# Q and K of a gated cross-attention layer kept in DRAM by units of a batch, and the bulk loads of its attention phase issued by ScalarE

## The chip, the cores and the metric

The kernel runs on one core of a Trainium2 chip. The metric is the time of one execution on the device, in microseconds. The kernel before takes 879.33 us, the median of 3 runs (877.48 to 880.64).

## The reference

A gated cross-attention layer and a feed-forward layer with LoRA experts, in float32: 8 batches of 128 tokens, width 512, 32 heads of 128.

```python
h = rmsnorm(layernorm(x)) * ln_weight                      # x: 8 x 128 x 512
q, k, v = h @ w_q.T, ctx @ w_k.T, ctx @ w_v.T              # each 8 x 128 x (32 heads x 128)
score = softmax(where(mask, q k^T + position_bias, -inf))  # per batch and head, 128 x 128
attn = (score v) @ w_out.T                                 # 4096 -> 512
x = x + tanh(g_xattn) * (layernorm(x) + attn)
n = layernorm(x)
x = x + tanh(g_ffn) * (n @ base_W.T + base_b + 2 * top-8 routed LoRA experts(n))
```

## The kernel before

Each float32 operand is split into a high and a low part, and a product is three matmuls (low x high, high x low, high x high). The work has three phases.

*Projections (0 to about 330 us).* 32 jobs (`JOBS`), 16 for K and 16 for Q, each for two heads. The first two are plain; in the others seven block products (`m1` to `m7`, 42 matmuls) make four quarters of a result, R11, R21, R12, R22, each for one head and one half of the batches. ScalarE makes the high part of a quarter in `unit_out`, VectorE the low part, and SyncE's `store(i, n)` (L320) writes it to `qk_units` in DRAM; `st[i]` counts these stores. There are 128 stores of 512 KB. One quarter holds, for each of the 128 partitions, 4 batches x 256 floats (high and low of 128 tokens).

*Attention (about 318 to 830 us).* 64 units: a unit is one batch with a group of 4 heads; unit t = 8g + b is batch b of group g. `load_unit(g, b)` (L353) fetches Q and K of a unit, 1 MB, into one of two buffers `qk`. TensorE's step for unit t makes the scores of t (8 matmuls into Sb), V of t+1 (12 matmuls), the output of t-4 (12), and applies the probabilities of t-2 to V (8 matmuls into Ab, which read `P_hl`). The probabilities are transposed by way of DRAM: VectorE normalises (`p_norm`) and transposes 32 x 32 blocks (`p_blocks`); `store_blocks` (L337) writes them to `p_rows`, `load_blocks` (L343) reads them back in four DMAs into `pT`; ScalarE and POOL split `pT` into `P_hl`. ScalarE's step for unit t (L795) is A_hi and small_a of t-3, V_hi of t, P_hl of t-2 (which waits for `pT`), one split of a weight chunk for the next group, and the four exponentials of t. `load_wv` and `load_wo` fetch W_v and W_o of the next group, one of eight chunks in each unit.

*Feed-forward (about 790 to 882 us).* It begins within the last group: VectorE and POOL make the second layer norm, and the weights (`loraR`, `loraB`, `base`) are split in `late_high` and `late_low`.

All engines are programmed in order, each by its own list, and wait on semaphores. All DMAs are issued by SyncE, in program order: for each unit it waits for p_blocks of t-1 and stores them, waits for the scores of t and loads unit t+2, waits for the stored rows and issues the four reads of `pT`, then one chunk of W_v or W_o. The first units have their own order (`first_units`, L406).

Of the kernel before, what the change touches and what calls it, by code (L numbers as in the profile page):

```python
# [13 lines left out]
P = 128  # L14
# [37 lines left out]
def build(nc, x, ctxT, mask, g_xattn, g_ffn, bias, lnw, wqk, wv, wo, baseT, base_b, loraR, router_b,  # L52
          lora_B, expert_map, qk_units, p_rows, out):
    with ExitStack() as ctx:
# [254 lines left out]

        @block.sync  # L310
        def _(sp):
# [8 lines left out]
            def store(i, n):  # L320
# [6 lines left out]
            def load_wv(g, q, k):  # L327
                if k == 0:
                    reached(sp, v_done, B * (g - 1))
                sp.dma_start(v_raw[q][:, k, :], wv[g, :, k, :]).then_inc(ld_wv[k], 16)  # L330

            def load_wo(g, q, k):
                if k == 0:
                    reached(sp, o_done, B * (g - 1))
                sp.dma_start(o_raw[q][:, k, :], wo[g, :, k, :]).then_inc(ld_o[k], 16)
# [13 lines left out]
            def load_bias(g, q):  # L349
                reached(sp, bm_done, B * (g - 1))  # L350
                sp.dma_start(bias4[:, q, :, :], bias[g, :, :, :]).then_inc(ld_bias, 16)
# [17 lines left out]
            load_bias(0, 0)  # L369
# [5 lines left out]
            for n in range(JOBS + 1):  # L375
# [5 lines left out]
                if n == 19:  # L381
                    for k in range(4):
                        sp.wait_ge(t_lo_done[k], 2)
                    for k in range(DC):
                        load_wv(0, 0, k)
                    for k in range(HU):
                        load_wo(0, 0, k)
                if n >= JOBS - 2 and n < JOBS:
# [3 lines left out]
                    load_unit(0, n % 2)  # L392
# [13 lines left out]
            def first_units():  # L406
                for i in range(4):
                    sp.wait_ge(st[i], 16 * (G + 2))
                sp.wait_ge(scores_done, 1)
                load_unit(0, 2)  # L410
                store_blocks(0, 0)
                load_blocks(0, 0)
                sp.wait_ge(scores_done, 2)
                load_unit(0, 3)
                store_blocks(0, 1)
                load_blocks(0, 1)
                sp.wait_ge(scores_done, 3)
                load_unit(0, 4)
                store_blocks(0, 2)
                load_blocks(0, 2)  # L420
                sp.wait_ge(m_done[4], J(JOBS - 1))
                load_wv(1, 1, 0)
                sp.wait_ge(scores_done, 4)
                load_unit(0, 5)
                load_wv(1, 1, 1)

            def group(g, q):
                first, last = (isinstance(g, int) and g == n for n in (0, GROUPS - 1))
                for b in range(4 if first else 0, B):
                    if first and b == 7:  # L430
                        for i in range(4):
                            sp.wait_ge(st[i], 16 * JOBS)
                    before = (g, b - 1) if b > 0 else (g - 1, B - 1)
                    store_blocks(*before)
                    if not (last and b >= B - 2):
                        sp.wait_ge(scores_done, B * g + b + 1)
                        load_unit(g + (b + 2) // B, (b + 2) % B)
                    load_blocks(*before)
                    if 2 <= b <= 5 and not last:
                        load_wv(g + 1, 1 - q, b - 2)  # L440
                    if b >= 6 and not last:
                        load_wo(g + 1, 1 - q, b - 6)
                    if b < 2 and not first:
                        load_wo(g, q, b + 2)
                    if b == (4 if first else 1) and not last:
                        load_bias(g + 1, 1 - q)
# [190 lines left out]
        def _(act):  # L637
# [205 lines left out]
            for n in range(PLAIN, JOBS + 1):  # L843
# [41 lines left out]
                if n == JOBS - 1:  # L885
                    exponentials(0)
# [916 lines left out]
```

## Time and profile before

| | |
|---|---|
| profiled execution | 884.5 us |
| its span, granted clock | 882.3 us, 0.984 |
| TensorE (PE) busy | 847.7 us (96%) |
| VectorE (DVE) busy | 699.9 us (79%) |
| ScalarE (ACT) busy | 494.7 us (56%) |
| GpSimd (POOL) busy | 496.1 us (56%) |
| DMA | 155392 packets, 214.72 MB, mean 243 GB/s |

PE counts as busy from the start of a matmul to its modelled end, and matmuls overlap; whether a stretch is tight is seen from the distance of their starts. The longest wait of any engine is ScalarE's before P_hl, for `pT`: 124.7 us in 60 times.

### The profile page before, as it was taken

What the parts mean: (1) busy time and instruction counts of PE and PEld (TensorE: products, weight loads), DVE (VectorE), ACT (ScalarE), POOL (GpSimd) and SP (SyncE); (2) the same over time, 40 slices, a digit from 0 to 9 for tenths busy, and PEclk for the clock granted to TensorE, in tenths of its full rate; (3) what the DMA queues carried; (4) which work ended last, traced back from release to release, by engine and by line L of the source; (5) the groups of instructions that cost most, each with busy time, mean ns of one, the idle gap of its engine ahead of it and who ended that gap; (6) DMA issues with size and microseconds to landing.
All of it is one profiled execution on the core that took longest, in us unless ns stands there. A gap on an engine that the chain in (4) does not pass through costs nothing.

```text
span 882.3 us, 13927 instructions
## 1 busy us (share of the span) xinstructions
PE 847.7 (96%) x4212; PEld 712.1 (81%) x4212; DVE 699.9 (79%) x1172; ACT 494.7 (56%) x1185; POOL 496.1 (56%) x352
## 2 busy tenths in 40 slices
PE   7999999999999998889999999999999999987898
PEld 5887888778888887778888888888888888876786
DVE  6888777877766666568888889889988989899664
ACT  6566776666676753456555555555555555546210
POOL 0353534653465532557576776777667666757422
PEclk9999999999999999899999999999999999999799
DMA  8876677579777785987988888898898898884001
GB/s 291 309 280 246 249 276 274 215 294 360 275 299 274 274 309 156 284 270 227 259 230 264 241 249 255 249 259 252 250 257 246 251 260 253 273 262 140 25 25 72
DMA packets 155392, 214.72 MB, mean 243 GB/s; under 512 B 10960, under 2 KB 109392, under 8 KB 154960
## 3 DMA queue, kind: packets, MB, share of 16 engines
q1 hardware_dynamic: 155344, 214.13, 75.6%
q8 instruction: 24, 0.39, 0.2%
q14 instruction: 24, 0.20, 0.1%
HBM read 128.11 MB, written 85.98 MB: 243 GB/s over the span
## 4 chain that ended last, share of the span: by engine, by line
PE 32%; DMA 24%; DVE 24%; ACT 7%; issue 5%; SPq 4%; POOL 1%; DVEq 0%; ACTq 0%; POOLq 0%
DMA pT<-p_rows 11%; DMA p_rows<-p_blocks 10%; DVE p_norm L1128 6%; PE Sb L1417 4%; PE Sb L1418 4%; PE Sb L1419 4%; ACT p_exp L773 4%; SPq L346 4%; DVE unit_out L950 2%; PE Ab L1417 2%; PE Ab L1418 2%; PE Ab L1419 2%; DVE p_blocks L1134 2%; DVE rscale L1123 2%; DMA v_raw<-wv 2%
## 5 line engine op out<-in xcount | busy, mean ns | idle before, releaser
L495 POOL TENSOR_TENSOR w_lo<-w_raw,w_hi 128x1280 fp32r<-128x1280 f32 (+1 forms) x29 | 84.8, 2924 | 122.7 <-ACT w_hi L639 122.7
L544 POOL TENSOR_TENSOR P_hl<-pT,P_hl 128x512 fp32r<-128x512 f32 x64 | 82.8, 1294 | 103.1 <-ACT P_hl L639 103.1
L539 POOL TENSOR_TENSOR a_rest<-small_a,A_hi 128x512 f32<-128x512 f32 x64 | 89.9, 1404 | 47.3 <-ACT small_a L767 47.1
L639 ACT ACTIVATE P_hl<-pT 128x512 fp32r<-128x512 f32 x64 | 40.5, 633 | 124.7 <-DMA pT<-p_rows 124.7
L773 ACT ACTIVATE p_exp<-s_sb,negmax 128x128 f32<-128x128 f32 x256 | 99.0, 389 | 10.2 <-DVE negmax L1105 9.7
L532 POOL TENSOR_TENSOR bm<-bias,maskneg 128x512 f32<-128x512 f32 x64 | 84.1, 1313 | 17.7 <-DVE s_sb L1111 11.9
L1128 DVE TENSOR_TENSOR p_norm<-p_exp,rscale 128x512 f32<-128x512 f32 x64 | 90.2, 1410 | 2.3
L1588 PE MATMUL Ab<-P_hl,V_hi 128*128 128x256 f32 x256 | 65.8, 335 | 17.6 <-POOL P_hl L544 14.4
L639 ACT ACTIVATE A_hi<-Ab 128x512 fp32r<-128x512 f32 x64 | 38.3, 598 | 67.9 <-PE Ab L1589 67.9
L639 ACT ACTIVATE U<-Sb 128x512 f32<-128x512 f32 x90 | 53.6, 600 | 40.5 <-PE Sb L1419 39.9
L639 ACT ACTIVATE w_hi<-w_raw 128x512 fp32r<-128x512 f32 (+2 forms) x67 | 60.2, 903 | 22.5 <-PE Kb L1419 6.7
L1417 PE MATMUL Sb<-t_hi,w_lo 128*128 128x512 f32 x180 | 70.5, 392 | 1.2 <-ACT U L639 1.2
L1588 PEld LDWEIGHTS Ab<-P_hl,V_hi 128*128 128x128 f32 x256 | 49.1, 192 | 26.8 <-POOL P_hl L544 24.9
L1419 PE MATMUL Sb<-t_hi,w_hi 128*128 128x512 f32 x180 | 70.1, 389 | 0.0
L1418 PE MATMUL Sb<-t_lo,w_hi 128*128 128x512 f32 x180 | 70.1, 389 | 0.0
L1564 PE MATMUL Sb<-qk 128*128 128x256 f32 x248 | 65.3, 341 | 1.4 <-DMA qk<-qk_units 1.4
L500 POOL TENSOR_TENSOR w_lo<-w_raw,w_hi 128x512 fp32r<-128x512 f32 x30 | 40.3, 1345 | 36.8 <-ACT w_hi L639 36.8
L950 DVE TENSOR_TENSOR unit_out<-Ob,unit_out 128x512 fp32r<-128x512 f32 x61 | 42.0, 688 | 22.2 <-ACT unit_out L639 21.8
L1589 PE MATMUL Ab<-P_hl,V_lo 128*128 128x128 f32 x256 | 57.7, 225 | 0.0
L1566 PE MATMUL Sb<-qk 128*128 128x128 f32 x248 | 56.0, 226 | 0.0
L1408 PE MATMUL Vb<-v_hi,c_lo 128*128 128x512 f32 x128 | 53.3, 416 | 2.9 <-POOL v_lo L518 1.4
L1134 DVE STREAM_TRANSPOSE p_blocks<-p_norm 128x512 f32<-128x512 f32 x64 | 45.6, 712 | 13.1 <-DVE p_norm L1128 10.1
(300 smaller groups left out, 2703.2 us busy)
## 6 DMA issues: line engine op xcount, KB each, us to landing
qk_units<-unit_out SPq DMA_DIRECT2D x128, 512.0 KB, 3.3
qk<-qk_units SPq DMA_DIRECT2D x64, 1024.0 KB, 7.3
p_rows<-p_blocks SPq DMA_DIRECT2D x64, 256.0 KB, 2.7
pT<-p_rows SPq DMA_DIRECT2D x256, 64.0 KB, 4.2
w_raw<-wqk SPq DMA_DIRECT2D x31, 512.0 KB, 4.3
v_raw<-wv SPq DMA_DIRECT2D x32, 256.0 KB, 4.8
o_raw<-wo SPq DMA_DIRECT2D x32, 256.0 KB, 4.7
stage<-ctxT SPq DMA_DIRECT2D x8, 256.0 KB, 5.7
```

What stands on the lines that cost most here:

```text
L495: pool.tensor_tensor(w_lo[:, n % 2, first:5, :], w_raw[:, n % 2, first:5, :], f32(w_hi[:, n % 2, first:5, :]), ALU.subtract).then_inc(w1_l ...
L532: pool.tensor_tensor(bm[:, :, :], bias4[:, q, :, :], maskneg[:, b:b + 1, :].broadcast_to([P, HU, S]), ALU.add).then_inc(bm_done, 1)
L539: pool.tensor_tensor(a_rest[:, :, :], small_a[:, :, :], f32(A_hi[:, r, :, :]), ALU.subtract).then_inc(a_rest_done, 1)
L544: pool.tensor_tensor(blocked(P_hl[:, :, 1, :]), queries(pT[:, r, :, :, :]), f32(blocked(P_hl[:, :, 0, :])), ALU.subtract).then_inc(p_lo_do ...
L639: act.activation(dst, src, ACT.Copy).then_inc(done, 1)
L773: last = act.activation(p_exp[:, i, :], s_sb[:, i, :], ACT.Exp, bias=negmax[:, i:i + 1], accum_out=rowsum[:, i:i + 1])
L1128: dve.tensor_tensor(p_norm[:, :, :], p_exp[:, :, :], scale, ALU.mult).then_inc(norm_done, 1)
L1417: pe.matmul(bank, lo, m_hi[:, c, :], start=first, stop=False, skip_group_check=not fresh)
L1418: pe.matmul(bank, hi, m_lo[:, c, :], start=False, stop=False, skip_group_check=not fresh)
L1419: last = pe.matmul(bank, hi, m_hi[:, c, :], start=False, stop=c == 1, skip_group_check=not fresh)
L1564: pe.matmul(Sb[:, h, :, :].rearrange("p a k -> p (a k)"), Q_hl[:, 0:S], K_hl, start=True, stop=False)
L1588: pe.matmul(Ab[:, h, :, :], V_hi[:, r, h, :], P_hl[:, h, :, :], start=True, stop=False)
```

## The change

`qk_units` has its batch dimension ahead of the heads. Before, a quarter was stored in one run of 4 KB per partition and a unit was loaded in eight runs of 1 KB per partition; now a quarter is stored in four runs of 1 KB (512 in all) and a unit is loaded in one run of 8 KB.

`load_unit` from unit 2 on, `load_wv` and `load_wo` from group 1 on, the later loads of the bias, and the loads of `loraR`, `loraB` and `base` are issued by ScalarE, between V_hi and P_hl of its step, with the waits that they had on SyncE. SyncE keeps the stores of quarters, `p_rows`, `pT` and `x_again`. The splits of `loraR`, `loraB` and `base` come one unit later, and those of the last two chunks of `base` behind the loop, on ScalarE and on POOL. The core of the diff (removed lines of SyncE's list are cut):

```diff
         @block.sync
-                sp.dma_start(qk_units[2 * (g // 2) + half, :, 2 * head + n // G, :, :],
+                sp.dma_start(qk_units[2 * (g // 2) + half, :, :, 2 * head + n // G, :],
                              f32(unit_out[:, i, :]).rearrange("p (b k) -> p b k", b=BH)).then_inc(st[i], 16)
...
-            def load_unit(g, b):
-                sp.dma_start(f32(qk[:, b % 2, :, :, :]).rearrange("p h a k -> p (h a) k"),
-                             qk_units[2 * g + b // BH, :, :, b % BH, :]).then_inc(ld_qk[b % 2], 16)
+        def load_unit(eng, g, b):
+            eng.dma_start(f32(qk[:, b % 2, :, :, :]).rearrange("p h a k -> p (h a k)"),
+                          qk_units[2 * g + b // BH, :, b % BH, :, :].rearrange("p c k -> p (c k)")).then_inc(
+                              ld_qk[b % 2], 16)
...
+            for b in range(3):
+                store_blocks(0, b)
+                load_blocks(0, b)
...
         @block.scalar
                 v_evict_hi(t, b)
+                if first and b == 7:
+                    for i in range(4):
+                        act.wait_ge(st[i], 16 * JOBS)
+                if not (last and b >= B - 2):
+                    act.wait_ge(scores_done, t + 1)
+                    load_unit(act, g + (b + 2) // B, (b + 2) % B)
+                if 2 <= b <= 5 and not last:
+                    load_wv(act, g + 1, 1 - q, b - 2)
+                if b >= 6 and not last:
+                    load_wo(act, g + 1, 1 - q, b - 6)
+                if b < 2 and not first:
+                    load_wo(act, g, q, b + 2)
+                if b == (4 if first else 1) and not last:
+                    load_bias(act, g + 1, 1 - q)
...
                 probs_hi(t - 2, b % 2, B // 2 * g + b // 2)
...
                 if n == JOBS - 1:
+                    for i in range(4):
+                        act.wait_ge(st[i], 16 * (G + 4))
+                    act.wait_ge(scores_done, 1)
+                    load_unit(act, 0, 2)
                     exponentials(0)
+                    act.wait_ge(scores_done, 2)
+                    load_unit(act, 0, 3)
...
+            act.wait_ge(scores_done, 3)
+            load_unit(act, 0, 4)
+            load_wv(act, 1, 1, 0)
             probs_hi(0, 0, 1)
...
+            act.wait_ge(scores_done, 4)
+            load_unit(act, 0, 5)
+            load_wv(act, 1, 1, 1)
             probs_hi(1, 1, 1)
...
-    args.append(nc.dram_tensor("qk_units", (2 * GROUPS, P, 2 * HU, BH, 2 * S), F32, kind="Internal").ap())
+    args.append(nc.dram_tensor("qk_units", (2 * GROUPS, P, BH, 2 * HU, 2 * S), F32, kind="Internal").ap())
```

SyncE's list before, from the load of unit 4 to p_rows of unit 3 (`qk` is the load of a unit, `p_rows` the store of a unit's blocks, `pT` its four reads):

```order
L354 DMA qk<-qk_units 128x8x256 [waits scores_done]
L340 DMA p_rows<-p_blocks 128x512 [waits blocks_done]
L346 DMA pT<-p_rows 32x4x128 [waits rows_done]
L346 DMA pT<-p_rows 32x4x128 x3
L330 DMA v_raw<-wv 128x512 [waits m4_done]
L354 DMA qk<-qk_units 128x8x256 [waits scores_done]
L330 DMA v_raw<-wv 128x512
L340 DMA p_rows<-p_blocks 128x512 [waits blocks_done]
```

And now, from p_rows of unit 2 to the store behind pT of unit 3:

```order
L350 DMA p_rows<-p_blocks 128x512 [waits blocks_done]
L356 DMA pT<-p_rows 32x4x128 [waits rows_done]
L356 DMA pT<-p_rows 32x4x128 x3
L350 DMA p_rows<-p_blocks 128x512 [waits blocks_done]
L356 DMA pT<-p_rows 32x4x128 [waits rows_done]
L356 DMA pT<-p_rows 32x4x128 x3
L344 DMA qk_units<-unit_out 512x1x256 [waits unit_lo_done]
```

The loads of the units and of W_v are gone from between the transfers of the probabilities. ScalarE's list before, from A_hi of unit 0 to the first split of the next group's W_v:

```order
L639 ACTIVATE A_hi<-Ab 128x512 [waits pv_done]
L767 ACTIVATE small_a<-Ab 128x512
L639 ACTIVATE V_hi<-Kb 128x512 [waits v_done]
L639 ACTIVATE P_hl<-pT 128x4x128 [waits pv_done,pt_done]
L773 ACTIVATE p_exp,rowsum<-s_sb,negmax 128x128 [waits norm_done,max_done]
L773 ACTIVATE p_exp,rowsum<-s_sb,negmax 128x128 x3
L639 ACTIVATE v_hi<-v_raw 128x512 [waits ld_c0_0]
```

And now:

```order
L604 ACTIVATE A_hi<-Ab 128x512 [waits pv_done]
L732 ACTIVATE small_a<-Ab 128x512
L604 ACTIVATE V_hi<-Kb 128x512 [waits v_done]
L326 DMA qk<-qk_units 128x2048 [waits scores_done]
L314 DMA v_raw<-wv 128x512
L604 ACTIVATE P_hl<-pT 128x4x128 [waits pv_done,pt_done]
L738 ACTIVATE p_exp,rowsum<-s_sb,negmax 128x128 [waits norm_done,max_done]
L738 ACTIVATE p_exp,rowsum<-s_sb,negmax 128x128 x3
L604 ACTIVATE v_hi<-v_raw 128x512 [waits ld_c0_0]
```

The load of unit 5 and the second chunk of W_v stand ahead of P_hl; the first chunk, which the split at the end waits for, is issued one P_hl earlier, ahead of these rows.

## Rows read from the trace of the kernel before

**Rows 1.** Busy time, clock and DMA of seven stretches (view by windows).

```profile
core 0: us, PE busy (x) PEld busy (x) DVE busy (x) ACT busy (x) POOL busy (x), PEclk, DMA share, GB/s
250.00:300.00 50.00, 50.00 (x223) 41.40 (x222) 31.99 (x59) 34.59 (x55) 29.21 (x16) 1.00 0.74 278
349.40:405.90 56.50, 50.84 (x241) 43.35 (x241) 37.86 (x60) 26.35 (x79) 32.06 (x25) 0.88 0.81 251
405.90:762.60 356.70, 354.27 (x1922) 304.31 (x1921) 315.13 (x479) 207.21 (x624) 249.35 (x192) 1.00 0.88 253
762.60:804.70 42.10, 37.98 (x203) 31.41 (x202) 39.56 (x58) 21.61 (x65) 26.57 (x20) 1.00 0.80 240
210.00:220.00 10.00, 10.00 (x46) 8.29 (x45) 7.24 (x15) 6.63 (x11) 4.22 (x2) 1.00 1.03 419
567.25:569.00 1.75, 1.75 (x9) 1.45 (x8) 1.75 (x4) 1.75 (x7) 1.35 (x2) 1.00 0.81 218
569.25:570.25 1.00, 1.00 (x9) 0.96 (x8) 0.51 (x3) 0.39 (x3) 1.00 (x2) 1.00 1.07 377
```

**Rows 2.** PE's timeline: start, duration, instruction, idle time before and its releaser.

```profile
327.00 0.40 PE L1417 MATMUL Sb<-t_hi,w_lo 128*128 128x512 f32 x1
331.10 0.28 PE L1564 MATMUL Sb<-qk 128*128 128x256 f32 x1
349.45 0.41 PE L1564 MATMUL Sb<-qk 128*128 128x256 f32 x1 [1.37 <-DMA qk<-qk_units]
360.30 0.58 PE L1588 MATMUL Ab<-P_hl,V_hi 128*128 128x256 f32 x1 [2.61 <-POOL P_hl L544]
396.00 0.39 PE L1588 MATMUL Ab<-P_hl,V_hi 128*128 128x256 f32 x1 [2.80 <-POOL P_hl L544]
405.88 0.33 PE L1564 MATMUL Sb<-qk 128*128 128x256 f32 x1
413.20 0.33 PE L1564 MATMUL Sb<-qk 128*128 128x256 f32 x1
```

**Rows 3.** SyncE's timeline: issues of DMAs in the first units and around unit 30.

```profile
329.96 3.11 SPq L346 DMA_DIRECT2D pT<-p_rows  x4
343.01 0.55 SPq L354 DMA_DIRECT2D qk<-qk_units  x1
350.05 1.73 SPq L346 DMA_DIRECT2D pT<-p_rows  x4
351.82 0.43 SPq L330 DMA_DIRECT2D v_raw<-wv  x1
565.30 0.34 SPq L340 DMA_DIRECT2D p_rows<-p_blocks  x1
568.03 1.75 SPq L346 DMA_DIRECT2D pT<-p_rows  x4
```

**Rows 4.** ScalarE's timeline: the handoff, the first units and around unit 30.

```profile
324.45 0.60 ACT L639 ACTIVATE U<-Sb 128x512 f32<-128x512 f32 x1 [0.22 <-PE Sb L1419]
334.58 0.63 ACT L639 ACTIVATE P_hl<-pT 128x512 fp32r<-128x512 f32 x1 [1.95 <-DMA pT<-p_rows]
355.80 0.63 ACT L639 ACTIVATE v_hi<-v_raw 128x512 fp32r<-128x512 f32 x1 [7.91 <-DMA v_raw<-wv]
563.90 0.60 ACT L639 ACTIVATE V_hi<-Kb 128x512 fp32r<-128x512 f32 x1
574.12 0.63 ACT L639 ACTIVATE P_hl<-pT 128x512 fp32r<-128x512 f32 x1 [1.93 <-DMA pT<-p_rows]
```

**Rows 5.** The chain of waits in the first units: start, us, what.

```profile
343.61 6.42 DMA p_rows<-p_blocks
380.27 4.69 DMA qk_units<-unit_out
```

**Rows 6.** DMA issues: count, KB each, median us from issue to landing.

```profile
p_rows<-p_blocks SPq DMA_DIRECT2D x64, 256.0 KB, 2.7
out<-p_exp SPq DMA_DIRECT2D x4, 256.0 KB, 2.0
```

More of the change, by code:

```diff
@@ L384, in _ @@
                     for k in range(DC):
-                        load_wv(0, 0, k)
+                        load_wv(sp, 0, 0, k)
                     for k in range(HU):
-                        load_wo(0, 0, k)
+                        load_wo(sp, 0, 0, k)
                 if n >= JOBS - 2 and n < JOBS:
@@ L391, in _ @@
                     sp.wait_ge(st[R21], 16 * (G + 2))
-                    load_unit(0, n % 2)
+                    load_unit(sp, 0, n % 2)
                 if n == JOBS:
@@ L404, in _ @@
                     store(R12, n - 1)
[L406 to L425, printed above, removed]
+            for b in range(3):
+                store_blocks(0, b)
+                load_blocks(0, b)
             def group(g, q):
@@ L429, in group @@
                 for b in range(4 if first else 0, B):
-                    if first and b == 7:
-                        for i in range(4):
-                            sp.wait_ge(st[i], 16 * JOBS)
                     before = (g, b - 1) if b > 0 else (g - 1, B - 1)
                     store_blocks(*before)
-                    if not (last and b >= B - 2):
-                        sp.wait_ge(scores_done, B * g + b + 1)
-                        load_unit(g + (b + 2) // B, (b + 2) % B)
                     load_blocks(*before)
[L439 to L446, printed above, removed]
-                    if first and b > 3 and b < 7:
+                    if first and b < 7:
                         store((R22, R21, R12)[b - 4], JOBS - 1)
@@ L457, in group @@
                         sp.dma_start(x_again[:, b % 2, :], x[:, b, :]).then_inc(ld_x2[b % 2], 16)
-                    if last and b == 3:
-                        sp.wait_ge(o_done, LAST)
-                        sp.dma_start(base_raw[:, :, :], baseT).then_inc(ld_base, 16)
-            first_units()
             group(0, 0)
@@ L573, in step @@
                     split_wo_lo(g + 1, 1 - q, 0)
-                if last and b == 3:
+                if last and b == 4:
                     late_low(0, loraR_lo, loraR_raw, loraR_hi)
-                if last and b == 4:
+                if last and b == 5:
                     late_low(1, w_loraB_lo, loraB_raw, w_loraB_hi)
-                if last and b >= 5:
-                    late_low(b - 3, w_base_lo[:, b - 5, :], base_raw[:, b - 5, :], w_base_hi[:, b - 5, :])
+                if last and b >= 6:
+                    late_low(b - 4, w_base_lo[:, b - 6, :], base_raw[:, b - 6, :], w_base_hi[:, b - 6, :])
             for n in range(PLAIN - 1, JOBS):
@@ L618, in _ @@
             late_root(3)
-            late_low(5, w_base_lo[:, 3, :], base_raw[:, 3, :], w_base_hi[:, 3, :])
+            for k in (2, 3):
+                late_low(2 + k, w_base_lo[:, k, :], base_raw[:, k, :], w_base_hi[:, k, :])
             a_remainder(UNITS - 2, 0)
@@ L800, in step @@
                 v_evict_hi(t, b)
+                if first and b == 7:
[12 more added lines that the diff above has]
+                    load_bias(act, g + 1, 1 - q)
+                if last and b == 2:
+                    act.wait_ge(v_done, LAST)
+                    act.dma_start(loraR_raw, loraR).then_inc(ld_lora, 16)
+                    act.dma_start(loraB_raw, lora_B).then_inc(ld_loraB, 16)
+                if last and b == 4:
+                    act.wait_ge(o_done, LAST)
+                    act.dma_start(base_raw[:, :, :], baseT).then_inc(ld_base, 16)
                 probs_hi(t - 2, b % 2, B // 2 * g + b // 2)
@@ L807, in step @@
                     split_wo_hi(g + 1, 1 - q, 0)
-                if last and b == 3:
+                if last and b == 4:
                     act.wait_ge(ld_lora, 16)
                     late_high(loraR_hi, loraR_raw)
-                if last and b == 4:
+                if last and b == 5:
                     act.wait_ge(ld_loraB, 16)
@@ L814, in step @@
                 exponentials(t)
-                if last and b >= 5:
+                if last and b >= 6:
                     act.wait_ge(ld_base, 16)
-                    late_high(w_base_hi[:, b - 5, :], base_raw[:, b - 5, :])
+                    late_high(w_base_hi[:, b - 6, :], base_raw[:, b - 6, :])
             plain_first_hi(0)
@@ L927, in _ @@
             y_hi(0)
-            late_high(w_base_hi[:, 3, :], base_raw[:, 3, :])
+            for k in (2, 3):
+                late_high(w_base_hi[:, k, :], base_raw[:, k, :])
             probs_hi(UNITS - 2, 0, UNITS // 2)
```

27 lines of the change are left out of this document (12 added, 15 removed).

## The prediction

> **What bounds the kernel now.** I read first the stages [rows 1]. [...] TensorE is busy for 96% of the span, so the question is which stretches are longer than their matmuls. In 250 to 300 us the projections run without a gap: 223 matmuls in 50 us, and 42 make a job of the projections, so a job is 9.4 us, with DMA at 0.74. In the attention phase a unit has 40 matmuls (8 for the scores, 12 for V, 12 for the output, 8 for the probabilities). From one unit's scores to the next is 413.20 - 405.88 = 7.32 us when nothing waits [rows 2]. Against this floor:
> - units 4 to 9, from 349.45 to 405.88 [rows 1, 2]: 56.4 us for six units (241 matmuls), 12.5 above 6 x 7.32 = 43.9. The clock is 0.88 on average. The two largest gaps, 2.61 and 2.80 us, wait for POOL's P_hl, and one of 1.37 us just before unit 4 waits for the load of qk [rows 2].
> - units 10 to 57, from 405.9 to 762.6: 1922 matmuls are 48 units, 351.4 us of floor in 356.7: only 5.3 above.
> - units 58 to 62, from 762.6 to 804.7: 42.1 us against 36.6, 5.5 above; VectorE is busy for 39.56 of these 42.1.
>
> So all that faster transfers can give back is 12.5 + 1.4 + 5.3 + 5.5 = 24.7 us, and over half of it stands in six units.
>
> I looked next at what those six wait for, in SyncE's timeline [rows 3] and ScalarE's [rows 4]. SyncE runs in program order, so it is itself a queue: the load of unit 4 is issued at 343.01, behind the wait for p_rows of unit 1, though its buffer was free once the scores of unit 2, which start at 331.10 and take 0.9, were done; PE waits for it at 349.45 [rows 2]. The first chunk of the next group's W_v is issued at 351.82, behind p_rows of unit 2. ScalarE comes to its split with 7.91 us of waiting and goes on at 355.80. Behind that split on ScalarE stand A_hi of unit 1, V_hi of unit 4 and P_hl of unit 2, and POOL's and PE's work on them; this makes the gap at 360.30 and the half clock behind it. And p_rows of unit 2, issued at 343.61 right behind 1 MB of qk on the same queue, lands only 6.42 us later, against a median of 2.7 [rows 5, 6]. At 380.27 SyncE waits 4.69 us for the last store of a unit before it issues p_rows of unit 6 [rows 5]; this makes the gap at 396.00.
>
> **The change, part by part.**
> *Loads issued by ScalarE, units 4 to 9.* Now the load of unit 4 comes when the scores of unit 2 are done and ScalarE is past its last unit_out (about 333), 10 us earlier, and W_v's chunk right behind it, 18 us earlier. The 1.37 us and the 7.91 us go. What is late next: P_hl of unit 2. Its p_rows can go at about 341 with nothing ahead of it on its queue; with 2 to 4.7 us for p_rows (below), 1.75 of issue and some 3 us of landing it is there by 348 to 351, while PE wants it at 354.4 (349.45 - 1.37 = 348.1 for the scores of unit 4, + 0.9 + 24 x 0.224 for the products, 0.224 being 50 us by 223). So the gap at 360.30 goes with the half clock behind it. The wait for all stores moves from SyncE to ScalarE, ahead of the load of unit 9. The last store is still issued by SyncE behind pT of unit 5, so ScalarE stands there for 0 to 3 us with P_hl of unit 5 and the exponentials of unit 7 behind it; p_rows of unit 6 no longer does. The sum of what can go is 12.5 + 1.4 = 13.9; I leave 2 for the wait for the stores and 1 for contention: -11 us (bounds -4, if only the waits of 1.37 and 2.61 at PE go, and -13.9).
>
> *Loads issued by ScalarE, steady units.* ScalarE issues at the end of V_hi, where it waits for pT anyway: V_hi of unit 31 ends at 563.90 + 0.60 = 564.50, and before P_hl at 574.12 the wait is 1.93 us [rows 4]. Two issues cost at most 0.55 + 0.43 = 0.98 us by SyncE's [rows 3], mostly hidden. The wait for the scores costs nothing, since PE has them done before V_hi ends. What changes is the order of the transfers. Now p_rows of unit 30 goes at 565.30, pT at 568.03 to 569.78, and pT lands at 574.12, 4.3 us after its last issue, because the 1 MB of qk stands between the two on one queue. Without it I bound pT's landing by unit 0: 333.07 to 334.58, 1.5 us. Against it stands p_rows: the load now starts about 0.8 us ahead of it. If the two queues share the engines, p_rows lands within 2.0 us (the stores of out, as large, in a quiet stretch [rows 6]) plus the whole 1 MB at 377 GB/s, 2.8 us, so 4.8 instead of 2.7. The chain from p_blocks to P_hl is thus 0.7 to 3.5 us shorter. It is worth only what PE waits, at most 5.3 us; ScalarE's own sequence (V_hi, two issues, P_hl, a split, then four exponentials) becomes about as late as VectorE's negmax, which keeps part of it. I take -3.5 (bounds +5, if the 0.98 us of issues come on top in one unit of ten, and -5.3).
>
> *Load in 8-KB runs.* The same bytes in 128 packets instead of 1024. A stretch with almost only 1-KB packets moves 377 GB/s at a share of 1.07, one with mostly 4-KB packets 419 at 1.03 [rows 1]: 352 against 407 GB/s for a full share, so the 1 MB takes 2.6 instead of 3.0 us of DMA time, in a share of 0.88 [rows 1]. This eases waiting and is within the term above.
>
> *Stores in 1-KB runs.* Each of the 128 stores, 0.52 MB, becomes 512 packets instead of 128 and its instruction reads 512x1x256. No row of before shows a 1-KB write. By the nearest rows, 2.1 MB a job take 5.2 us at 407 GB/s and 6.0 us at 352: the share rises from 0.74 to 0.83, no job becomes longer, 0 us. The other end is the first part of a 1-KB load, 218 GB/s at 567.25 [rows 1]: then 9.6 us of stores and 1.3 us of weights would stand against 9.4 us, +1.5 for each of 29 jobs, +44 us. I take 0, since the slow part is seen only at the start of loads.
>
> [...]
>
> *Handoff.* ScalarE's U of job 31, at 324.45 before [rows 4], now stands behind a wait for the scores of unit 1 and an issue. PE has six V matmuls between these scores and its next use of U at 327.00 [rows 2], so the scores end at 327.00 - 6 x 0.224 = 325.7, and U is there at 325.7 + 0.55 + 0.60 = 326.8: in time for PE, 2.4 us later for VectorE, which has p_blocks of unit 0 ahead of it anyway. 0 (to +2.4).
>
> *Last group.* The splits of the late weights move one unit on, and two splits of base stand behind the loop: ScalarE's (0.6 us) ahead of P_hl of unit 62, POOL's ahead of a_rest, which waits for ScalarE's small_a. 0. Of the 5.5 us VectorE holds most; an earlier W_o load and pT give 1: -1 us (0 to -3).
>
> Sum: -11 - 3.5 - 1 = -15.5 us. Against the profiled execution's 884.5 us (span 882.3) this is 869.0. It is 5.2 above the median of the timed runs, 879.33. Part of that excess may be the very start stall that goes, so I take off a little less than the whole: 865 us.
>
> **Rivals.**
> 1. *Only the order of issues counts.* The 1 MB on the second queue holds p_rows up as much as it did pT, and nothing comes of the steady units; the start gives 7 to 8. For it: 5.3 us is little, and the same engines carry both queues. Against it: the worst sum above is still 0.7 us shorter. About 872. [...]
> 2. *Slower: the 1-KB stores bound the projections.* Place: each job of the first 318 us. It decides once 2.1 MB no longer fit in 9.4 - 1.3 = 8.1 us, below 259 GB/s. For it: 218 GB/s in the first 1.75 us of a 1-KB load. Against it: 377 right behind. Price up to +44: 865 + 44 = 909; at 240 GB/s +0.64 a job, 884.
> 3. *No difference.* ScalarE, held by its issues and by the wait for the stores, loses what the transfers give. For it: the wait for the stores moves onto the engine whose P_hl PE waits for. Against it: 2 us of idle time in nearly every unit. 878 to 881.
>
> **How the numbers follow.** Forecast 0.57 (856 to 869), rival 1 0.18 (869 to 876), rival 2 0.17, rival 3 0.08. Within 0.3% is 876.7 to 882.0, about what a measurement can tell here. Faster: 0.57 + 0.18 = 0.75; same 0.08; slower 0.17. The range reaches from 854 (nearly all of the 24.7 us) to 884 (rival 2 at 240 GB/s); some 0.15 is left out, nearly all above. The likeliest case's own range is 856 to 869.
>
> **What would show it.** Units 4 to 9 take 44 to 48 us and the clock there is above 0.95; ScalarE no longer waits for v_raw for 8 us. ScalarE's wait for pT before P_hl is mostly gone. pT lands in about 2 to 3 us after its issue and p_rows in 3 to 4.5. In 250 to 300 us PE stays without a gap and DMA is near 0.83 at 278 GB/s. Wrong it would be if a job becomes longer than 9.4 us, if PE waits in the steady units more than now, or if ScalarE stands long at the stores before unit 9's load.

## The result, and the profile after

The change made the kernel slower. The changed kernel takes 944.12 us (median of 4 runs, 931.15 to 953.36) where the kernel before took 879.27 beside it (877.48 to 880.64): a ratio of 1.066, 95% interval 1.057 to 1.076. The ratio takes only the two faster executions of the changed kernel (931.15 and 943.10), since the other two were over 1.5% above its fastest. The forecast was 865, with a range of 854 to 884. The profiled execution took 945.15 us, with a span of 942.9.

The windows of the changed kernel, cut where those of before were (250 to 300 us of the projections, then units 4 to 9, 10 to 57, 58 to 62); columns as in [rows 1]:

```profile
250.00:300.00 50.00, 50.00 (x222) 41.44 (x221) 32.17 (x60) 34.59 (x55) 27.96 (x16) 1.00 0.86 281
353.50:410.00 56.50, 46.61 (x243) 39.67 (x242) 37.98 (x62) 26.30 (x79) 31.58 (x26) 0.96 0.72 238
410.00:828.50 418.50, 374.45 (x1922) 319.56 (x1921) 308.15 (x481) 207.04 (x624) 250.55 (x193) 0.95 0.65 215
828.50:870.60 42.10, 38.43 (x203) 33.27 (x202) 35.89 (x58) 21.23 (x64) 24.95 (x19) 0.96 0.69 223
```

Read against [rows 1], the loss stands in one row. Units 10 to 57 take 418.5 us instead of 356.7 for the same 1922 matmuls: +61.8 us, where the span grew by 60.6. The rest: units 2 and 3 +2.9, the start of unit 2 +1.2 (332.3 instead of 331.1), units 4 to 9 and 58 to 62 nothing, and the part that begins with unit 63's scores -5.3. Of the 61.8, PE's idle time is 44.1 instead of 2.4, +41.6; its busy time is 374.5 instead of 354.3, +20.2, for matmuls at the half clock behind those gaps (granted clock 0.50 from 470.83 to 473.81, behind a gap of 3.62 us: a matmul of 128x256 took 0.52 us there, and 0.34 at 1.00 at 460.08). The projections keep 50.00 of 50.00. The DMA engines were busy for 0.65 of the slow stretch instead of 0.88, and moved 215 GB/s instead of 253: they were not short of bandwidth on average (run 10 below moves 257 GB/s in the same units without a gap).

The waits of the changed kernel: engine and line, what it waits for, total us, times, longest.

```profile
POOL P_hl L508 <- ACT P_hl L604: 138.0, 54, 7.2
ACT P_hl L604 <- DMA pT<-p_rows: 134.0, 39, 7.5
PEld Ab L1587 <- POOL P_hl L508: 74.5, 25, 5.1
ACT P_hl L604 <- issue: 21.3, 20, 4.3
```

It is one chain: DMA, ScalarE's P_hl, POOL's P_hl, PE. The wait for pT was 124.7 us in 60 times before and should have gone; now it is 134.0 in 39, and longest 7.5. (The last row, `issue`, is idle time before P_hl that no semaphore explains; ScalarE's own issues of DMAs lie in it.) The DMA issues of the changed kernel, columns as in [rows 6]:

```profile
qk<-qk_units ACTq DMA_DIRECT2D x62, 1024.0 KB, 5.4
p_rows<-p_blocks SPq DMA_DIRECT2D x64, 256.0 KB, 5.7
pT<-p_rows SPq DMA_DIRECT2D x256, 64.0 KB, 2.0
```

p_rows went from 2.7 to 5.7. The median of pT fell to 2.0 (4.2 before), and yet the wait for it grew, since it ends with the last of four reads. The reason is seen in the chain of waits of the changed kernel over one stretch (start, us, what; rows between are left out at the dots):

```profile
454.30 0.72 DVE p_blocks L1133
455.04 5.79 DMA p_rows<-p_blocks
...
462.14 6.35 DMA pT<-p_rows
...
469.05 0.61 ACT o_hi L604
469.66 1.55 ACT p_exp L738 x8
...
471.77 1.74 DVE p_norm L1127
...
473.70 0.72 DVE p_blocks L1133
474.44 5.99 DMA p_rows<-p_blocks
...
481.75 5.76 DMA pT<-p_rows
...
493.48 4.67 DMA p_rows<-p_blocks
```

p_rows, pT, P_hl, a split, the exponentials of the unit two later, p_norm, p_blocks, p_rows: a closed loop, in which each step waits for the one before it, once round in two units. Here one round is 474.44 - 455.04 = 19.40 us, the next 19.04; PE needs 2 x 7.32 = 14.64. These are two of the long rounds; the 24 rounds of units 10 to 57 average 418.5 / 24 = 17.44.

Before, the same round began with the store at 565.30 [rows 3], P_hl at 574.12 [rows 4], and ended with this row of SyncE's timeline of the kernel before:

```profile
580.10 0.34 SPq L340 DMA_DIRECT2D p_rows<-p_blocks  x1
```

That is 8.82 us to P_hl and 5.98 from there: 14.80, already 0.16 above PE's 14.64 (356.7 / 24 = 14.86 on average). In the changed kernel P_hl stands at 468.51, 13.47 us behind the store, and 5.93 follow. In this round the whole loss is in the two transfers. Over the 48 stores of units 10 to 57, from the start of the store's issue to P_hl it took 10.84 us on average instead of 8.93, and the store was issued 0.47 us behind the end of p_blocks instead of 0.04, since SyncE often still stood at the pT reads of the unit before; from P_hl to the end of p_blocks two units later it was 6.08 and 6.07.

What lies beside them: SyncE's issues of the changed kernel,

```profile
439.34 0.36 SPq L350 DMA_DIRECT2D p_rows<-p_blocks  x1
441.82 2.77 SPq L356 DMA_DIRECT2D pT<-p_rows  x4
446.75 0.34 SPq L350 DMA_DIRECT2D p_rows<-p_blocks  x1
449.53 1.73 SPq L356 DMA_DIRECT2D pT<-p_rows  x4
455.04 0.34 SPq L350 DMA_DIRECT2D p_rows<-p_blocks  x1
460.85 1.73 SPq L356 DMA_DIRECT2D pT<-p_rows  x4
```

and ScalarE's in the same stretch:

```profile
439.60 0.34 ACTq L326 DMA_DIRECT2D qk<-qk_units  x1
446.93 0.34 ACTq L326 DMA_DIRECT2D qk<-qk_units  x1
454.24 0.34 ACTq L326 DMA_DIRECT2D qk<-qk_units  x1
454.67 0.39 ACTq L319 DMA_DIRECT2D o_raw<-wo  x1
461.56 0.37 ACTq L326 DMA_DIRECT2D qk<-qk_units  x1
468.51 0.63 ACT L604 ACTIVATE P_hl<-pT 128x512 fp32r<-128x512 f32 x1 [6.34 <-DMA pT<-p_rows]
```

At 439 and 446 the load is issued 0.26 and 0.18 us behind the store, and pT's reads, which wait for the store, begin 2.48 and 2.78 us after it. At 454 the load is 0.80 us ahead of the store, and pT's reads begin 5.81 us after it. Then the next load, at 461.56, comes in the middle of pT's four issues (460.85 to 462.58), and P_hl starts 5.9 us after the last of them. Over units 6 to 59 of this trace the load was issued ahead of the store 42 times of 54, and from the end of the store's issue to the first pT read 5.46 us passed on average (4.1 to 6.6). Of the 12 times behind, the ten that were 0.18 us or more behind took 1.7 to 3.4; the two that were 0.05 and 0.15 behind took 5.2. So in this trace tenths of a microsecond, in who is first, decide about 3 us.

What the DMA engines did in that time is told by the packets of the two queues, q1 (SyncE's) and q10 (ScalarE's): number, MB and share of the engines' time. The store is 128 packets of 2 KB, the load 128 of 8 KB, and the weight chunk issued at 454.67 again 128 of 2 KB. First from the load's issue at 454.24 to 458.90, and from there to 460.84, when the store had landed:

```profile
q10 hardware_dynamic: 199, 1.16, 74.5%
```

```profile
q1 hardware_dynamic: 144, 0.26, 35.5%
q10 hardware_dynamic: 89, 0.15, 20.5%
```

In the first stretch q1 has no row: for 3.86 us after its issue not one packet of the store was moved. The whole load (1.05 MB) and some of the chunk went first, and the store with the rest of the chunk. Where the load is 0.18 us behind it is the other way round, here from the store's issue at 446.75 to 448.25 (q1's packets include the last of the pT reads before):

```profile
q1 hardware_dynamic: 139, 0.21, 47.4%
q10 hardware_dynamic: 10, 0.02, 2.9%
```

At 773.99, with the load 0.15 us behind, the store had begun when the load's packets came, and its rest was moved slowly among them: from 775.50 to 778.50 q10 moved 125 packets, 0.97 MB, and q1 68, 0.11 MB.

### The profile page after: what moved, and what is told of

It is laid out like the page before. It is cut to its first block, busy times and chain, and to the rows that moved or that the text cites. A ratio compares the mean times of both kernels' runs of the same rounds, so it can differ in the third digit from the quotient of the medians.

```text
span 942.9 us, 13924 instructions
## 1 busy us (share of the span) xinstructions
PE 863.1 (92%) x4212; PEld 723.9 (77%) x4212; DVE 687.1 (73%) x1172; ACT 494.5 (52%) x1185; POOL 497.3 (53%) x352
## 4 chain that ended last, share of the span: by engine, by line
PE 48%; DVE 15%; DMA 14%; issue 11%; ACT 5%; POOL 5%; SPq 2%; ACTq 0%; DVEq 0%; POOLq 0%
DMA p_rows<-p_blocks 7%; DMA pT<-p_rows 6%; PE Sb L1416 4%; PE Sb L1417 4%; PE Sb L1418 4%; PE Ab L1587 3%; DVE unit_out L949 2%; ACT p_exp L738 2%; DVE p_norm L1127 2%; PE Sb L1563 2%; POOL a_rest L503 2%; PE Ab L1416 2%; PE Ab L1417 2%; PE Ab L1418 2%; PE Kb L1407 2%
## 5 line engine op out<-in xcount | busy, mean ns | idle before, releaser
L1587 PE MATMUL Ab<-P_hl,V_hi 128*128 128x256 f32 x256 | 67.8, 342 | 64.6 <-POOL P_hl L508 63.6
L604 ACT ACTIVATE P_hl<-pT 128x512 fp32r<-128x512 f32 x64 | 40.4, 632 | 157.6 <-DMA pT<-p_rows 134.0
L738 ACT ACTIVATE p_exp<-s_sb,negmax 128x128 f32<-128x128 f32 x256 | 99.2, 389 | 23.7 <-DVE negmax L1104 23.2
L496 POOL TENSOR_TENSOR bm<-bias,maskneg 128x512 f32<-128x512 f32 x64 | 83.7, 1309 | 17.9 <-DVE s_sb L1110 12.8
L604 ACT ACTIVATE A_hi<-Ab 128x512 fp32r<-128x512 f32 x64 | 38.3, 599 | 99.2 <-PE Ab L1588 99.1
L1120 DVE RECIPROCAL rinv<-rowsum 128x4 f32<-128x4 f32 x64 | 11.3, 177 | 100.1 <-ACT p_exp L738 99.7
L1127 DVE TENSOR_TENSOR p_norm<-p_exp,rscale 128x512 f32<-128x512 f32 x64 | 79.7, 1246 | 2.2
L604 ACT ACTIVATE U<-Sb 128x512 f32<-128x512 f32 x90 | 53.6, 600 | 42.9 <-PE Sb L1418 40.4
L1563 PE MATMUL Sb<-qk 128*128 128x256 f32 x248 | 71.4, 364 | 0.0
L1565 PE MATMUL Sb<-qk 128*128 128x128 f32 x248 | 59.0, 238 | 0.0
```

The lines of the kernel that those rows point to most:

```text
L496: pool.tensor_tensor(bm[:, :, :], bias4[:, q, :, :], maskneg[:, b:b + 1, :].broadcast_to([P, HU, S]), ALU.add).then_inc(bm_done, 1)
L604: act.activation(dst, src, ACT.Copy).then_inc(done, 1)
L738: last = act.activation(p_exp[:, i, :], s_sb[:, i, :], ACT.Exp, bias=negmax[:, i:i + 1], accum_out=rowsum[:, i:i + 1])
L1127: dve.tensor_tensor(p_norm[:, :, :], p_exp[:, :, :], scale, ALU.mult).then_inc(norm_done, 1)
L1563: pe.matmul(Sb[:, h, :, :].rearrange("p a k -> p (a k)"), Q_hl[:, 0:S], K_hl, start=True, stop=False)
L1587: pe.matmul(Ab[:, h, :, :], V_hi[:, r, h, :], P_hl[:, h, :, :], start=True, stop=False)
```

## The experiments

Times are medians, set against the kernel before on the same chip (882 to 883 us there); "p_rows 2.2" and the like are medians from issue to landing, from the profile's list of DMA issues.

**1. The layout alone.** The kernel before with the new layout; all issues as before.

```
-  qk_units[2*(g//2)+half, :, 2*head+n//G, :, :]      (store)
+  qk_units[2*(g//2)+half, :, :, 2*head+n//G, :]
-  qk_units[2*g+b//BH, :, :, b%BH, :]                 (load, 8 x 1 KB)
+  qk_units[2*g+b//BH, :, b%BH, :, :]                 (load, 8 KB)
```

> Only the layout of qk_units changes (1-KB stores, 8-KB loads); SyncE issues everything in the order of before. Theory Q (a load on the second queue gets ahead of p_rows, whatever its packets): p_rows lands in 2.7 us as before, pT in 3.9 to 4.2, time 872 to 880 us. Theory P (8-KB packets by themselves hold small ones up): on one queue p_rows goes ahead of the load, so it is unhurt too, 872 to 880; pT behind the load no later than before. Theory S (1-KB stores cost time): over 885 us, with gaps of PE before 300 us. If the layout alone explains the loss: 930 or more.

870.11 us (865.55 to 873.62), ratio 0.986 (0.981 to 0.991): faster by 1.4%, and below the 872 to 880 that was expected, since shorter landings of p_rows and pT had not been expected. Its windows, its issues and ScalarE's wait for pT:

```profile
250.00:300.00 50.00, 50.00 (x222) 41.42 (x221) 32.17 (x60) 34.57 (x54) 28.15 (x16) 1.00 0.86 281
348.50:401.90 53.40, 47.03 (x242) 40.27 (x242) 36.91 (x61) 26.98 (x82) 31.54 (x25) 0.94 0.82 262
```

```profile
qk<-qk_units SPq DMA_DIRECT2D x64, 1024.0 KB, 5.3
p_rows<-p_blocks SPq DMA_DIRECT2D x64, 256.0 KB, 2.2
pT<-p_rows SPq DMA_DIRECT2D x256, 64.0 KB, 3.4
```

```profile
ACT P_hl L639 <- DMA pT<-p_rows: 34.3, 21, 4.6
```

The 1-KB stores leave the projections gapless. The load of a unit lands in 5.3 us instead of 7.3, pT and p_rows gain 0.8 and 0.5, ScalarE's wait for pT falls from 124.7 to 34.3, and units 10 to 57 take 351.6 us: the floor. The layout gives all that the change could give in the steady units; what costs 74 us (944.12 - 870.11) is in the rest of the change.

**2. The issuing alone.** The changed kernel with the old layout (the diff of run 1 reversed).

> The changed kernel with the old layout: 4-KB stores, loads in 1-KB runs, issued by ScalarE. Theory Q: p_rows still lands in 5 us or more, time 925 to 950 us. Theory P: 1-KB packets let those of the other queue in between, p_rows lands in 3 to 3.5 us and the time falls to 875 to 895. Theory C (ScalarE is held up by its issues and waits, not by DMA): same as the changed kernel, 935 to 950, with p_rows near 5.7 as there.

959.98 us (948.42 to 971.22), ratio 1.079 (1.072 to 1.086). p_rows 4.3, pT 4.2, the load 7.5; the wait for pT is 160.6 us. The time is above every range that was expected, and p_rows lies between those of theories P and Q. The loss doesn't need 8-KB packets. The four kernels make a square: the issuing costs 77.0 us with the old layout and 74.0 with the new one, and the layout gives 12.9 and 15.9 (the changed kernel's time is from the other set of runs, where the kernel before took 879.27).

**3. and 4. The load behind the pT reads, on SyncE alone**, with the old layout (e3) and the new one (e4).

```
   store_blocks(*before)
-  wait scores_done; load_unit(...)
   load_blocks(*before)                 # the pT reads
+  wait scores_done; load_unit(...)
```

> The kernel before with one exchange in SyncE's list: in each step from unit 4 on the load of a unit stands behind the four reads of pT instead of ahead of them. Theory Q: only the order on the queue counts; pT then lands in about 2 us, the next p_rows comes 3 us later with the load mostly gone (2.7 to 3.5 us), PE's waits for P_hl in the steady units go, 870 to 877 us. If a load behind pT reaches into the next p_rows: as long as before or up to 5 us longer.

> The exchange of the run before this one together with the new layout. Theory Q: the load takes 2.6 instead of 3.0 us or more, so it is gone before the next p_rows: 866 to 875 us. Theory P: a p_rows behind 8-KB packets still on the engines lands later than in the run with 1-KB packets.

1052.87 us (1051.72 to 1056.47), ratio 1.193, and 958.49 (954.50 to 961.97), ratio 1.086. I had expected a gain, since pT would be free of the load, and it was: 1.9 us. But p_rows takes 6.7 us in e3 (5.0 in e4, so the 8-KB packets do not hold it longer there):

```profile
538.25 0.55 SPq L354 DMA_DIRECT2D qk<-qk_units  x1
538.98 0.52 SPq L330 DMA_DIRECT2D v_raw<-wv  x1
540.19 0.34 SPq L340 DMA_DIRECT2D p_rows<-p_blocks  x1
546.52 1.74 SPq L346 DMA_DIRECT2D pT<-p_rows  x4
```

"Behind pT(t-1)" is "just ahead of p_rows(t)". A second wait arose, too: ScalarE's for the weight chunks, 159.7 and 154.7 us in e3, and it stands between P_hl and the exponentials, inside the loop. My account was then that this wait was a good part of the loss; run 12 tests it.

**5. Only the weights on ScalarE.** The changed kernel with the unit loads back on SyncE, behind the store of p_rows as before.

```
 (SyncE)   store_blocks(*before)
+          wait scores_done; load_unit(sp, ...)
           load_blocks(*before)
 (ScalarE) - wait scores_done; load_unit(act, ...)
```

> The changed kernel with the 62 loads of units back on SyncE at their old places (between the store of p_rows and the pT reads); weight chunks, bias and the late weights stay on ScalarE. Theory A (what costs is the 1-MB load that ScalarE can issue ahead of p_rows and beside the pT reads; a chunk is a quarter of it): p_rows 2.2 to 3.0 us, pT 3.4 to 4, ScalarE's wait for pT before P_hl under 60 us, time 866 to 880 us. Theory B (any bulk on a second queue holds SyncE's small transfers, whatever its size or moment): p_rows stays above 4 us, time above 910 us.

874.11 us (870.16 to 884.23), ratio 0.988 (0.984 to 0.991). p_rows 3.6, above the 2.2 to 3.0 of theory A, and the wait for pT 83.8 instead of under 60; but the time is A's. Theory B falls: with a quarter of a megabyte on the second queue a store takes 1.4 us more (3.6 against 2.2 in run 1), and units 10 to 57 take 354.0 us against 351.6.

**6. ScalarE issues after P_hl.** The changed kernel, ScalarE's block of issues moved down by one instruction.

```
   v_evict_hi(t, b)
-  [load_unit, load_wv / load_wo, load_bias]
   probs_hi(t - 2, ...)
+  [load_unit, load_wv / load_wo, load_bias]
```

> The changed kernel with ScalarE's issues (load of unit t+2, weight chunk, bias) moved behind P_hl(t-2) instead of ahead of it, so that pT(t-2) has landed before the load is issued. Theory A (the moment counts, not the engine): p_rows 2 to 3.5 us, the wait for pT under 60 us, time 866 to 885 us. Theory B (the second queue as such costs): p_rows and pT as in the changed kernel (5.7 and 2.0 with 134 us of waiting), time 930 us or more. Theory C (the load is then late for the scores of t+2, or meets p_rows(t)): waits of the tensor engine for qk above 20 us, time 880 to 930 us.

873.00 us (867.27 to 880.07), ratio 0.985 (0.977 to 0.993).

```profile
p_rows<-p_blocks SPq DMA_DIRECT2D x64, 256.0 KB, 2.1
```

Same engine, same queue, same bytes: 71 us less than the changed kernel by a later place, with p_rows at 2.1. The wait for pT is 93.6 us, more than expected, and pT's median is 4.7, for which the loads, now issued just ahead of the next pT reads or beside them, are the likely cause; units 10 to 57 take 358.3 us, 7 above the floor. The second queue as such isn't the cause.

**7. The changed kernel with an eighth of the bytes.** ScalarE loads 1 KB per partition of units 2 to 63 instead of 8; seven eighths of these units' Q and K are left out.

> The changed kernel with ScalarE's loads of units 2 to 63 cut to one eighth of their bytes (1 KB per partition; the rest of each unit is not loaded). All issues, their order and their waits stay. Theory A (the bytes of the load that lie in the DMA engines ahead of p_rows and pT cost the time): p_rows about 2 us, time 855 to 870 us. Theory B (ScalarE's issuing or the waiting of its queue costs, not the bytes): time stays above 920 us.

859.52 us (857.27 to 862.32), ratio 0.969. p_rows 2.3, pT 2.2, units 10 to 57 in 351.4 us. The issues, their order and their waits are all there and PE has no gap in these units, though ScalarE's `issue` time before P_hl is 31.8 us in 54 times (21.3 in 20 in the changed kernel). In the ten units of 10 to 57 in which the small load was ahead of the store all the same, 2.5 us passed on average to the first pT read, where the changed kernel had 5.4. So it is the bytes, and not ScalarE's own issuing.

**8. Layout, and a better start on SyncE.** In units 0 to 8 each load behind the store and ahead of the pT reads, as later; the first W_v chunk a unit earlier; the wait for the last job's stores behind the store of p_rows(6).

```
   load(2); store_rows(0); [+ load(3)]; read_pT(0); [- load(3)]
   store_rows(1); [+ load(4)]; read_pT(1); [+ wv(1,1,0)]; [- load(4)]
   store_rows(2); [+ load(5)]; read_pT(2); [- wv(1,1,0), load(5)]; wv(1,1,1)
```

> The new layout with all issues on SyncE, and in units 0 to 8 the same order as later: each load of a unit right behind the store of p_rows and ahead of the pT reads; the first W_v chunk one unit earlier; the wait for the last job's stores behind the store of p_rows(6) instead of ahead of it. With the layout alone the tensor engine stands 8.2 us in three gaps between units 2 and 9 (1.5, 4.7, 2.0 us). If the order of these issues is their cause: 860 to 866 us, below the layout alone (870). If the start is bound by the dependent chain whatever the order: 868 to 872.

865.75 us (860.55 to 870.00), ratio 0.976 (0.969 to 0.982): within the 860 to 866 that was expected, and the fastest complete kernel here by its median. Units 4 to 9 take 49.2 us instead of 53.4. It doesn't stand clearly below run 1, though: their intervals overlap, and in the profiles its end, from unit 63's scores on, took 77.6 us against 72.3.

**9. One queue, the load ahead of p_rows.** Run 1 with two statements of SyncE exchanged.

```
+  wait scores_done; load_unit(...)
   store_blocks(*before)
-  wait scores_done; load_unit(...)
   load_blocks(*before)
```

> Layout alone with everything on SyncE, as before, but from unit 4 on each load of a unit is issued ahead of the store of p_rows instead of behind it (as soon as the scores of t are done). One queue, so nothing of a second queue is in it. Theory A (a 1-MB load issued ahead of p_rows costs, on whichever queue): p_rows 5 to 6.5 us instead of 2.2, time 910 to 960 us. Theory B (only two queues compete; in one queue it costs little): p_rows under 4 us, time 866 to 885 us.

1057.02 us (1050.94 to 1059.85), ratio 1.196 (1.191 to 1.202). p_rows takes 7.6 us:

```profile
512.62 0.33 SPq L354 DMA_DIRECT2D qk<-qk_units  x1
513.00 0.42 SPq L340 DMA_DIRECT2D p_rows<-p_blocks  x1
520.34 1.76 SPq L346 DMA_DIRECT2D pT<-p_rows  x4
523.32 0.42 SPq L340 DMA_DIRECT2D p_rows<-p_blocks  x1
```

Theory A's direction, and well past its 960: from 870 to 1057 us by one exchange. Not all of it is the store's landing in the loop of two units. From store to P_hl it took 10.90 us on average over units 10 to 57, hardly more than the changed kernel's 10.84, for pT is free here (1.9), and yet the time is 113 us longer. The rows show a second loop, SyncE's own list: it stands until the store has landed, issues the reads, a chunk and the next load, and only then the next store, 10.32 us after the last one, where PE needs 7.32 for a unit. The store is issued 2.24 us behind the end of p_blocks on average, against 0.07 in run 1. So this run shows what a load ahead of it does to the store, but its time is not a measure of that alone.

**10. ScalarE waits for p_blocks first.** The changed kernel with one more wait.

```
   act.wait_ge(scores_done, t + 1)
+  act.wait_ge(blocks_done, t)
   load_unit(act, ...)
```

> The changed kernel in which ScalarE, at the same place of its program, first waits until p_blocks(t-1) is written, the event at which SyncE issues the store of p_rows(t-1); so the load of unit t+2 can no longer be ahead of that store by more than the start of the two issues. Theory A (ScalarE's issue wins by some tenths of a microsecond to microseconds and this lead is the cost): p_rows 2 to 4 us, time 866 to 890 us. Theory B (the load beside p_rows costs as much as ahead of it, since 8-KB packets share the engines with 512-byte packets at once): p_rows 4.5 to 6 us, time 915 to 950 us.

877.28 us (868.95 to 881.35), ratio 0.994 (0.990 to 0.998). SyncE's and ScalarE's issues, and the windows of units 10 to 57:

```profile
450.15 0.34 SPq L350 DMA_DIRECT2D p_rows<-p_blocks  x1
452.39 1.76 SPq L356 DMA_DIRECT2D pT<-p_rows  x4
```

```profile
450.52 0.34 ACTq L326 DMA_DIRECT2D qk<-qk_units  x1
```

```profile
405.40:756.70 351.30, 351.30 (x1922) 304.83 (x1921) 324.38 (x481) 205.51 (x624) 244.80 (x193) 1.00 0.76 257
```

This is the closest experiment: nothing is moved or left out, a wait is *added*, and 67 us go. The load follows the store by 0.2 to 0.5 us in 47 of the 48 units, the store lands in 2.4 (median), and PE has no gap in them. Theory A holds, B (beside is as bad as ahead) falls. (That theory speaks of 512-byte packets; those are pT's: from 452.3 to 456, with the four reads, q1 moved 267 packets, 0.13 MB. The store's have 2 KB.) The chunk and the load's bytes are all there, and ScalarE's `issue` time before P_hl is 30.8 us.

**11. Run 8's loads with the weights on ScalarE behind P_hl.**

```
 run 5, and: loads of units 2 to 5 and the wait for the stores as in run 8;
 (ScalarE) - load_wv / load_wo / load_bias; probs_hi(t - 2, ...)
           + probs_hi(t - 2, ...); load_wv / load_wo / load_bias
```

> New layout; loads of units on SyncE behind the store of p_rows, from the first unit on, and the wait for the last job's stores behind the store of p_rows(6); weight chunks, bias and late weights on ScalarE behind P_hl(t-2). It joins what was best in the start (865.75 with all on SyncE) with the end of the changed kernel, whose gaps of the tensor engine were shorter. If the gaps of the end follow the late weights' issues: 861 to 865 us. If the chunks on a second queue meet p_rows or pT: 866 to 874 us.

877.16 us (869.72 to 883.89), ratio 0.992 (0.988 to 0.995): a miss. The start is the best of all complete kernels (units 4 to 9 in 48.6 us), but units 10 to 57 take 364.0 where run 8 takes 351.4; p_rows is 2.8, pT 3.9. The chunks come between the load and pT there, and ScalarE waits 99.2 us for pT. That these two go together the run shows; that the first makes the second I only argue.

**12. Run 4 with the weight chunk ahead of the load.**

```
   load_blocks(*before)
+  [load_wv / load_wo, load_bias]
   wait scores_done; load_unit(...)
-  [load_wv / load_wo, load_bias]
```

> The kernel that issues each load behind the pT reads on SyncE, with the new layout (958.5 us), but with the weight chunk and bias ahead of the load instead of behind it. If ScalarE's wait for the chunk (110 to 112 us each of waiting for W_v and W_o there) is what the exchange cost: those waits under 20 us and a time of 880 to 925 us. If the store of p_rows(t), issued behind the load (5.0 us there), is the cost: p_rows stays at 5 to 6 us and the time above 930 us.

1062.08 us (1059.94 to 1065.10), ratio 1.203, 104 us slower than run 4. The chunk's place was not the cause: ScalarE still waits 87.8 and 83.7 us for the chunks, and p_rows now goes right behind the load and takes 7.6 us instead of 5.0. My account of runs 3 and 4 falls; in these runs the time follows what stands directly ahead of p_rows. As in run 9 the next store is also held by SyncE's own list, 2.32 us behind p_blocks on average (0.12 in run 4).

## Why the prediction was wrong, point by point

- **Steady units, the failed step** (forecast -3.5, bounds +5 and -5.3; measured +61.8). The text saw the load coming 0.8 us ahead of p_rows, then bounded p_rows "within 2.0 us plus the whole 1 MB at 377 GB/s, 2.8 us, so 4.8", and pT by unit 0 at 1.5, and concluded that the chain from p_blocks to P_hl would be 0.7 to 3.5 us shorter. Three things were wrong in it. (a) The bound was none: with the load ahead of it a store took 5.46 us on average and up to 6.6, its issue not counted. It counted 1 MB ahead of the store, but the weight chunk was issued there, too, and its 0.26 MB went partly ahead of the store and partly beside it; at the same 377 GB/s it makes 0.7 us more, 5.5 by this estimate, near the median of 5.7. (b) pT was taken as free of the load. The load had left SyncE's order, and nothing kept the next one off the pT reads: 461.56, in the middle of them, and the last read landed 6.35 us after its issue. Both transfers were hit, once each by two different loads: 13.47 us to P_hl where 8.82 were. This was the larger error: from the end of the last read's issue to P_hl it took 3.77 us on average over units 10 to 57 (4.26 before), where 1.5 had been put in. (c) The chain was cut off at P_hl. Followed on through the exponentials to the next p_rows but one it was 14.80 us in the kernel before, against PE's 14.64. ScalarE's 1.93 us of waiting before P_hl [rows 4], which I read as room, is time of this loop, not slack. With no slack in it, +4.6 us makes a round of 19.4. On average the transfers took 1.9 us and SyncE's later issue 0.4 of the 2.6 by which a round grew; 24 rounds are the 61.8. PE's half clock did not set them: from P_hl to p_blocks the time is as before (6.08 and 6.07 us).
- **Why it stays slow** (argued from the rows). The load is released by the scores and V_hi, the store by the exponentials. In the rows above the loads come 7.3 us apart (439.60, 446.93, 454.24, 461.56), at PE's pace, while the third store comes 8.29 us behind the second: so the load got ahead. Once the loop is late, the scores are not as late, so the load is mostly ahead again, and the store late again. Run 10 breaks just this, by making the load wait for the loop, and PE runs 48 units without a gap. The kernel before had it by program order: the load stood behind the store on SyncE.
- **Units 4 to 9** (forecast -11; measured 0.0: 56.5 us before and after). The named waits went: PE's for qk, ScalarE's 7.91 us for v_raw. In their place PE waits for P_hl as in the steady units, 3.79 us and then half-clock matmuls (0.52 us at a granted clock of 0.50, from 372.50 to 374.00, where they take 0.33 at 1.00):

```profile
371.23 0.39 PE L1587 MATMUL Ab<-P_hl,V_hi 128*128 128x256 f32 x1 [3.79 <-POOL P_hl L508]
372.49 0.52 PE L1563 MATMUL Sb<-qk 128*128 128x256 f32 x1
```

  That the room was there shows run 8, at 49.2 us by earlier issues on SyncE, and run 7, at 45.8.
- **8-KB loads** (within the term above). Right, and larger than thought: a load lands in 5.3 us instead of 7.3, and the layout alone (run 1) took the steady units to 351.6 us (-5.1, near the bound of -5.3). It is the gain that I had laid to the order of issues.
- **1-KB stores** (0; rival 2 up to +44). Right: no job grew; the DMA share rose from 0.74 to 0.86 where 0.83 was forecast.
- **Handoff** (0 to +2.4). The scores of unit 2 start 1.2 us later, but 1.0 later in run 1, too, which has SyncE's issues; so at most 0.2 is ScalarE's. (The bound of 2.4 set the end of one U against the start of the other; start against start the same sum gives 1.8.) Units 2 and 3, which no term held, took 2.9 us more; they take 21.0 us in run 10, too, whose added wait begins behind them, and 16.8 in runs 6 and 7, so it is again the place and the bytes of the first loads.
- **Last group** (-1). 42.1 us before and after; with p_rows on time it was 36.6 in run 6, but 42.9 in run 10, so p_rows doesn't set it.
- **The rivals.** Rival 1 had the mechanism, "the 1 MB on the second queue holds p_rows up as much as it did pT", and 0.18; it was priced at 872 by the same bound of 4.8. That the same engines carry both queues is seen in the changed kernel: q10 alone took 90.0% of the time of all 16 from 455.04 to 458.90, and from 459 to 460 q1 took 59.2% and q10 33.0%. Issues from ScalarE gained nothing over run 1 in runs 6 and 10 (873.00 and 877.28 against 870.11), and in the changed kernel, where one engine's order is given up, they cost 74 us (944.12). Rival 3, ScalarE held by its issues, is answered by runs 7 and 10, where they are all there and PE has no gap in units 10 to 57. No rival let a load issued early lie ahead of both small transfers of the loop, and the chance of 0.17 for slower was all for the stores.

Still open: by what rule the DMA engines choose between two queues. The packets show a load that was issued first, at 454.24, moved whole ahead of the store (1.05 MB), and 54 pairs of one trace show how little lead that takes, but not why, nor where between 0.15 and 0.18 us it turns. And the part from unit 63's scores on took 72.3 us in the changed kernel at a clock of 0.95, and 77.6 before at 0.91; run 1, whose end is that of before, has 72.3 as well, so this is not the change's.

## What to carry to other kernels

Before a bulk transfer goes to another queue, find the loop of dependent small transfers that it shares the engines with, follow it all the way round, and compare one round with what PE needs in that time: idle time inside the loop is slack only as far as one round is shorter than that. Look at the issuing engine's own list in the same way, for it is a loop, too, where it waits for a landing (10.32 us from store to store in run 9, where PE needs 7.32). With the load behind the store on one queue p_rows took 2.2 us in run 1 (median); where that place is given up, let the bulk load wait for the event that releases the small one (run 10), or stand behind the instruction that needs it (run 6). Make the transfers cheaper first (here longer runs, 13 us less of measured time), and take order as a second, separate change.

## What the runs showed of the hardware

- A 256-KB store took 2.1 and 2.4 us (medians of runs 6 and 10) where a 1-MB load was issued on another queue, mostly 0.2 us or more behind it, and 5.7 in the changed kernel, where the load is mostly ahead; with the load ahead on the same queue 7.6 us (run 9).
- A store issued 0.80 us behind a load of another queue had no packet moved for 3.86 us, while 1.16 MB of that queue were (the changed kernel, 455.04 to 458.90; the MB from 454.24 on).
- The load held the store back with packets of either length: 4.3 us for p_rows with 1-KB packets (run 2), 5.7 with 8-KB ones, but 2.3 with an eighth of the bytes (run 7).
- Stores in 1-KB runs went at 281 GB/s, loads of the stretch included, without a gap, at a share of 0.86 where 4-KB writes took 0.74 (250 to 300 us, the changed kernel and the one before).
